# Order of VectorE's first scans, second input product and last statistics in a selective-scan and expert kernel

## The reference, cut to what matters

```
h = layernorm(x) * (1 + ca) + sa             # x: 2 x 2048 x 256
xn = layernorm(h, ln_w, ln_b)                # the "second statistics" are those of h
y  = mamba(xn, forward) and mamba(flip(xn), backward), 512 inner channels, 16 states:
     xp, z = split(xn @ W_in.T)
     xc = silu(conv4(xp) + b_conv)
     dt, B, C = split(xc @ W_x.T);  dt = softplus(dt @ W_dt.T + b_dt)
     s[t] = s[t-1] * exp(dt[t] * A) + (dt[t] * xc[t]) * B[t]      # the scan
     y[t] = sum over states of s[t] * C[t];  y = (y + xc * D) * silu(z);  out = y @ W_out.T
x = x + ga * (h + 0.5 * (y_forward + y_backward))
x = x + gb * experts(layernorm(x) * (1 + cb) + sb)     # 8 experts, 2 for each token, and a shared part
```

## Time and profile before

| | |
|---|---|
| median of 3 runs | 2089.03 us (2088.35 to 2089.89) |
| profiled execution, its own time | 2088.25 us |
| its span | 2086.5 us |
| VectorE busy | 1931.4 us, 93% |
| GpSimd busy | 1790.4 us, 86% |
| TensorE busy | 1814.2 us, 87% |
| ScalarE busy | 1590.2 us, 76% |

### The profile page before, as it was taken

The page is one execution under the profiler, slowest core; times in us unless marked ns, Lnnn a source line. Parts: engine busy times, 40 slices in busy tenths (PEclk is TensorE's granted clock), DMA queues, the critical chain, the costliest instruction groups (busy, mean ns, idle before and its releaser), DMA issues.

```text
span 2086.5 us, 25331 instructions
## 1 busy us (share of the span) xinstructions
PE 1814.2 (87%) x6766; PEld 826.6 (40%) x6766; DVE 1931.4 (93%) x1839; ACT 1590.2 (76%) x3343; POOL 1790.4 (86%) x607
## 2 busy tenths in 40 slices
PE   7888898979898888889898989898967499999997
PEld 3323332324242323233332323242312155669996
DVE  7999999999999999999999999999999977747776
ACT  5786879898989888776789898989887534346664
POOL 5689999999999999999999999999999824335555
PEclk9999898989898989989898989898978599999999
DMA  7746454454535362635454544535361493235554
GB/s 269 247 115 152 106 136 107 118 131 110 130 106 121 105 153 74 160 89 141 103 136 114 128 118 119 126 104 131 85 146 49 134 327 130 89 105 87 93 97 75
DMA packets 140222, 264.26 MB, mean 127 GB/s; under 512 B 21377, under 2 KB 43905, under 8 KB 138929
## 3 DMA queue, kind: packets, MB, share of 16 engines
q1 hardware_dynamic: 125488, 240.90, 43.5%
q0 software_dynamic: 13296, 17.80, 5.0%
q10 hardware_dynamic: 1296, 3.93, 0.5%
HBM read 193.36 MB, written 70.26 MB: 126 GB/s over the span
## 4 chain that ended last, share of the span: by engine, by line
PE 26%; ACT 21%; DVE 19%; POOL 17%; issue 15%; DMA 1%; DVEq 0%; ACTq 0%; POOLq 0%; SPq 0%
DVE hst L1671 11%; POOL hst L979 11%; ACT psum L1296 8%; PE psum L2275 5%; DVE dbu L1650 4%; POOL dbu L967 4%; PE psum L2362 3%; PE psum L2117 3%; PE psum L2371 3%; PE psum L2382 3%; ACT dbu L1328 3%; PE psum L2288 3%; PE psum L2037 1%; ACT sp_tmp L1265 1%; ACT dt L1260 1%
## 5 line engine op out<-in xcount | busy, mean ns | idle before, releaser
L979 POOL TENSOR_TENSOR hst<-hst,c_rep 128x2048 f32<-128x2048 f32 x254 | 1145.9, 4540 | 3.6 <-ACT state L1282 3.5
L1296 ACT ACTIVATE psum<-dt_rep,neg_a 128x512 f32<-128x512 f32 (+1 forms) x1024 | 659.8, 676 | 126.8 <-DVE hst L1671 122.4
L1671 DVE TENSOR_TENSOR_SCAN hst<-psum,state,dbu 128x1024 f32<-128x1024 f32 x264 | 604.1, 2328 | 0.0
L1671 DVE TENSOR_TENSOR_SCAN hst<-psum,dbu 128x1024 f32<-128x1024 f32 x248 | 555.1, 2270 | 8.8 <-ACT psum L1296 8.3
L1650 DVE TENSOR_TENSOR dbu<-psum,b_rep 128x2048 f32<-128x2048 f32 x176 | 398.2, 2263 | 5.7 <-PE psum L2102 5.6
L967 POOL TENSOR_TENSOR dbu<-dtu_rep,b_rep 128x2048 f32<-128x2048 f32 x80 | 364.3, 4554 | 11.7 <-DVE hst L1671 6.6
L2117 PE MATMUL psum<-hst,same 128*32 128x512 f32 x2048 | 273.5, 682 | 60.6 <-POOL hst L979 55.0
L2102 PE MATMUL psum<-dt,same 32*128 32x512 f32 x352 | 216.3, 696 | 108.6 <-DVE dbu L1650 100.0
L2049 PE MATMUL psum<-xp,taps 128*128 128x512 f32 x512 | 237.2, 606 | 6.6 <-ACT sp_tmp L1262 6.1
L1086 POOL DMA_INDIRECT out_x<-h,target_u x71 | 110.9, 1562 | 115.8 <-issue 69.5
L1328 ACT ACTIVATE dbu<-first_decay,dbu,state 128x1 f32<-128x1 f32 x504 | 160.0, 376 | 27.2 <-DVE dbu L1650 21.4
(11 more groups left out here) (194 smaller groups left out, 2571.1 us busy)
## 6 DMA issues: line engine op xcount, KB each, us to landing
dt_rep<-dt_scratch SPq DMA_DIRECT2D x256, 256.0 KB, 4.8
dtu_rep<-dtu_scratch SPq DMA_DIRECT2D x320, 64.0 KB, 1.9
taps<-taps_scratch SPq DMA_DIRECT2D x64, 256.0 KB, 4.4
b_rep<-bc_scratch SPq DMA_DIRECT2D x64, 256.0 KB, 4.8
c_rep<-bc_scratch SPq DMA_DIRECT2D x64, 256.0 KB, 7.8
dt_scratch<-dt SPq DMA_DIRECT2D x48, 256.0 KB, 6.0
h<-slot_scratch SPq DMA_DIRECT2D x71, 129.5 KB, 2.5
sp_tmp<-t_scratch SPq DMA_DIRECT2D x16, 512.0 KB, 6.7
```

Of the source, the lines that this page charges most:

```text
L979: nc.gpsimd.tensor_tensor(h, h, c_rep[q % 2][:], ALU.mult).then_inc(prod_done, 1)
L1296: nc.scalar.activation(psum[:, PS_A + i, kept], dt_rep[:, G % 2, j, kept], ACT.Exp, scale=neg_a[:, q % 2, u, i:i + 1]).then_inc(exp_done, 1)
L1671: nc.vector.tensor_tensor_scan(both(hst[:, U % RING, groups, :]), both(psum[:, PS_A + 2 * pair:PS_A + 2 * pair + 2, :]), both(dbu[:, U % D ...
```

## The change

The last block's `statistics(1, LAST)` moves from the end of the loop over blocks to behind `multiply(0)`. For unit 0 VectorE now scans both halves first and makes the input product of unit 1 afterwards. The round of unit 1 starts, as before, with the input product of unit 2. Nothing is added or taken away, and no other engine's program is touched.

```diff
             for n in range(NBLK):
                 statistics(0, n)
                 modulate(n)
-                statistics(1, n)
+                if n < LAST:
+                    statistics(1, n)
...
             multiply(0)
+            statistics(1, LAST)
 
             for T in range(ALL_UNITS):
                 q, t = divmod(T, UNITS)
+                if T == 0:
+                    scan(0, 0)
+                    scan(0, 1)
+                    multiply(1)
+                    continue
                 if T + 1 < ALL_UNITS and not on_pool(T + 1):
                     multiply(T + 1)
```

## The result

The changed kernel takes 2097.60 us (median of 6, 2095.51 to 2098.68) against 2089.11 us before (median of 6, 2088.35 to 2090.08). The ratio is 1.004, with a 95% interval of 1.003 to 1.0051. It is slower by 8.5 us, which is twice the 4.2 us that I had called measurable, and above my range (2087.3 to 2092.4). The profiled execution took 2095.51 us, 7.26 us more than the one before; its span is 2093.7 us, 7.2 us more.

The account below looks back on a forecast made before the run. VectorE and GpSimd were taken as full once the scans run, TensorE's order as the bound at the start. 0.95 us gained and 2.4 lost to half clock made +1.5, so 2090.5 us as a median; range 2087.3 to 2092.4.

Parts of the forecast that it names:

- VectorE's times up to the product of unit 2: VectorE's start: product of unit 0 at 72.65, first scan 77.1, product of unit 1 81.5, of unit 2 84.95 or 85.9.
- the wait that changes its place: VectorE's 2.16 us wait ahead of unit 1's product exchanged for 1.1 to 2.1 us ahead of unit 2's.
- the cover of the statistics: GpSimd gets last block's power and shift 2.4 us later, at no cost, since it waits until 81.61 for a transfer.
- TensorE's new gap: TensorE, ahead of the spread of unit 2: waits 3.5 us, until 83.85, for VectorE's product of unit 1.
- the fall of the clock behind it: TensorE's clock drops to half on the spread of unit 2 and the convolutions, losing 2.4 us; bounds 0 to 4.3.
- the chain's delay there: TensorE's chain through the convolutions of block 1: -0.95 + 2.4 = +1.5 us, passed on without slack.
- GpSimd's first input product: On GpSimd, it can start at 82.9 instead of 85.97 us, which is no gain by itself.
- the first part: Opening on what bounds the kernel: with VectorE and GpSimd full, a lead or delay from the start reaches the end unchanged.
- The sum: Whole kernel: -0.95 + 2.4 = +1.5 us on the profiled 2088.25, giving 2089.75, or 2090.5 us as a median.
- the gap of 1.87 us: TensorE's gap before 100.81 us, cited as leaving the clock at 1.00, while gaps above 2.7 us led to half.
- D: Clearly slower: half clock holds long behind the new gap, 10.3 us of chained work to pass +4.2 us; chance 0.04.
- B: GpSimd and ScalarE's 3 to 4 us in hand absorb the delay; median 2089.0; chance 0.17, shared with another rival.

Follow-up runs that it names:

- after_c: The changed kernel plus assertions that GpSimd's table values loaded in the last stage are within bounds; 2109.27 us.
- before_c: The kernel before plus assertions that GpSimd's table values loaded in the last stage are within bounds; 2101.23 us.
- after_fill: The changed kernel with constant waits in the tail, plus two unread TensorE products ahead of the transposes of block 6; 2236.69 us.
- before_k: The kernel before with another tail: GpSimd's last scatters wait for constant counts instead of loaded ones; 2233.87 us.
- longer_conv2: before_k with two taps of TensorE's first convolution of block 1 multiplied once more and overwritten, 1.8 us extra work; 2238.24 us.
- stats_moved_k: before_k with only the last statistics moved behind the input product of unit 0, scans as before; 2232.98 us.
- before_k2: before_k again, unchanged, in more rounds; median 2234.20 us.
- both_filled: The changed kernel with constant waits in the tail, first convolution ahead of the spread of unit 2, and two unread products ahead of block 6's transposes; 2237.99 us.
- stats_moved: before_c with only the last statistics moved behind the input product of unit 0, scans as before; 2099.88 us.
- scans_first: before_k with only both scans of unit 0 moved ahead of the input product of unit 1, statistics as before; 2234.67 us.
- conv_ahead: after_c with TensorE's convolution of block 1, chunk 0 placed ahead of the spread of unit 2; 2102.03 us.
- longer_conv4: before_k with four taps of TensorE's first convolution of block 1 multiplied once more and overwritten, 3.6 us extra work; 2238.57 us.

## Why the prediction was wrong

**Right.** VectorE's times up to the product of unit 2, each within 0.2 us; the wait that changes its place; the cover of the statistics (GpSimd's `step_input` came at 80.37 and waited for its transfer as before); TensorE's new gap (3.84 us, forecast 3.5); the fall of the clock behind it; and the chain's delay there, +2.0 us where I had +1.5. Its two parts were both larger than forecast: half clock cost 3.2 us on the spread and the convolution (2.07 + 5.78 against 1.05 + 3.63), not 2.4, and the spread began 1.16 us earlier than before (83.66 against 84.82), not 0.95. GpSimd's first input product came at 81.60 and not at 82.9, since its transfer landed sooner. None of that takes the time out of my range.

**The step that failed** stands in the first part: "whatever the start delivers late or early is carried to the end". Between units 3 and 16 it is not so: the delay grew from 2.0 to 8.7 us, of which 6.9 remained at the last unit. From unit 24 on it held to 0.2 us in this pair of traces (7.05 and 6.85), but not in all: after_c is 6.2 us behind before_c at unit 24, 7.8 at unit 40 and 6.8 at the last; after_fill is 4.0 behind before_k at unit 24 and 5.7 at the last. The sum priced one gap. But the first step has further gaps of TensorE, of 1.88 us ahead of the transposes of block 6, of 2.8 to 4.5 us around 130 and 160 us, of 0.99 us at 178.8, each of which can put half clock on chained work or not, and which do differed between the traces. I had used the gap of 1.87 us as proof that such a gap is harmless. It was one sighting; in the changed kernel, in longer_conv2 and in stats_moved_k half clock followed the same gap, and 2.6 to 2.8 us were lost between units 3 and 5 each time. after_fill shows that term by removing it. longer_conv2 shows that it doesn't need the new order, and before_k2, where the gap was 1.99 us long, the clock 0.52 from 100.0 to 103.5 us and the convolution took 5.40 us, that it doesn't need any edit at the start. So chance has a part in it too. But 2.6 us were lost there in all three traces of the changed kernel, and of the four of the kernel before only before_k2 lost anything, 0.7 us.

**The rivals.** D, clearly slower, got 0.04, and is what came, by another mechanism than the one written: not one long stretch at half clock behind the new gap, but three more stretches behind other gaps. I had the means to see it: half clock behind gaps at 133 and 158.5 us was among my rows, and I had used them as durations to borrow and not as places that could be hit again. B, absorption, is refuted for the first 16 units; 1.6 to 1.8 us were given back between units 16 and 24.

**What stays open.** The 3 us that arise between units 12 and 16 are read from the traces, behind a third gap at half clock, and weren't tested by themselves. They appear in the changed kernel, after_fill, both longer_conv kernels and both_filled, but also in stats_moved and before_k2, whose last unit is not late. With both tested gaps closed the changed order was still 3.8 us above the kernel before by medians, so the rival that the new order costs something by itself is not ruled out; against it stand scans_first and conv_ahead, each 0.8 us above. Nor is it shown why the last unit starts within 0.2 us in four traces of the kernel before and within 0.9 us in three of the changed one, although their stretches at half clock fall differently. What is shown is where the first 4.6 us come from, 2.0 behind the new gap and 2.6 behind the old one; how much of the 6.9 us at the end is theirs is not.

## What to carry to other kernels

When a reordering lets TensorE run ahead and then wait, price the gap by the clock behind it, and not only by its length; work of TensorE's own that can stand in the gap is worth more than the shortest wait. When a stage has several gaps like those here (1.9 to 4.5 us) on the chain, don't assume that a delay in it is carried unchanged: add to the range, for every gap behind the change, what half clock on the work behind it would cost. And one trace in which the clock held through a gap says little about the next execution, even of the same kernel.

## What the runs showed of the hardware

Behind the same gap of 1.87 or 1.88 us ahead of the same transposes the granted clock stayed at 1.00 in the kernel before, in stats_moved and in longer_conv4 and fell to 0.50 in the changed kernel, longer_conv2 and stats_moved_k. The place of the falls also differs between executions of one kernel: the kernel before with the constant waits was at half clock from 76.5 to 83 us in one trace, and from about 69.5 to 76 and again from 100.0 to 103.5 us in another. It started unit 3 at 100.59 in the first and at 98.20 in the second, and yet the last unit at 1654.54 and 1654.63. The page TensorE: Matmul & The Clock Gate of the Trainium skill, section "What's actually happening", says that the moment of a flip isn't tied to the kernel's start; these two traces agree: the falls at 76.5 and at about 69.5 lie 7 us apart.
